# Attention stage of a two-layer local-attention kernel: VectorE instructions issued without a wait for their own completion

## The reference

```python
def _layer(x, wqkv, qs, ksc, wo, lg, lb, w1, b1, w2, b2):
    h = shift_token(x)
    q, k, v = jnp.split(h @ wqkv, 3, axis=-1)      # to 8 heads of 64
    q = l2norm(q) * qs; k = l2norm(k) * ksc
    q, k = rotary_xpos(q, k)
    o = local_attention(q, k, v)                   # softmax(q k^T + mask) v
    x = x + o @ wo
    h = layernorm(shift_token(x)) @ w1 + b1
    a, g = jnp.split(h, 2, axis=-1)
    return x + (a * gelu(g)) @ w2 + b2
```

## Time and profile before

| | us |
|---|---|
| median of three runs | 2925.17 |
| lowest, highest | 2924.01, 2929.32 |
| the profiled execution, its own time | 2930.93 |
| its span on the slowest core (core 4) | 2929.4 |
| spans of the eight cores | 2912.0 to 2929.4 |
| TensorE busy | 2051.2 (70%) |
| VectorE busy | 1078.7 (37%) |
| ScalarE busy | 590.3 (20%) |

### The profile page before, as it was taken

The page is one execution under the profiler, slowest core; times in us unless marked ns, Lnnn a source line. Parts: engine busy times, 40 slices in busy tenths (PEclk is TensorE's granted clock), DMA queues, the critical chain, the costliest instruction groups (busy, mean ns, idle before and its releaser), DMA issues.

```text
span 2929.4 us, 27366 instructions; the slowest of 8 cores (2912.0 to 2929.4 us)
## 1 busy us (share of the span) xinstructions
PE 2051.2 (70%) x9366; PEld 931.7 (32%) x9488; DVE 1078.7 (37%) x1849; ACT 590.3 (20%) x1016; POOL 35.5 (1%) x50
## 2 busy tenths in 40 slices
PE   1167576799775674999225777758997767659993
PEld 1122232344322341444112233323442333314442
DVE  5705445311135446111373344453111444462113
ACT  1132331210022322110012233302100323311100
POOL 0000000000010000000000000000000000000000
PEclk9986556799885556999557855568998755579996
DMA  4239930121259800222332300001213200002223
GB/s 94 72 46 101 111 46 29 36 80 55 46 67 111 96 11 26 72 65 72 115 108 37 43 1 1 1 29 51 75 58 41 36 1 1 1 29 72 63 73 109
DMA packets 123852, 159.70 MB, mean 55 GB/s; under 512 B 48211, under 2 KB 90708, under 8 KB 122500
## 3 DMA queue, kind: packets, MB, share of 16 engines
q0 software_dynamic: 30624, 52.42, 15.4%
q1 hardware_dynamic: 93092, 105.53, 12.6%
HBM read 201.95 MB, written 44.03 MB: 84 GB/s over the span
## 4 chain that ended last, share of the span: by engine, by line
PE 60%; DVE 20%; ACT 6%; issue 5%; DMA 5%; SPq 3%; DVEq 1%; ACTq 0%
PE psA L1627 11%; PE psA L1185 8%; DVE UN L337 8%; PE psA L1610 5%; PE psA L1606 5%; PE psB L1610 5%; PE psB L1606 5%; DVE Bb L337 4%; DVE attnT L337 4%; PE psB L963 4%; PE psA L874 4%; PE psB L1224 3%; DMA out<-UN 2%; PE psA L1337 2%; PE psB L874 2%
## 5 line engine op out<-in xcount | busy, mean ns | idle before, releaser
L337 ACT ACT_TABLE_LOAD x67 | 86.0, 1283 | 1170.3 <-PE psA L1185 369.1
L1610 PE MATMUL psB<-stg,WS 128*128 128x512 bf16 x704 | 277.0, 393 | 24.6 <-ACT stg L337 23.2
L1606 PE MATMUL psB<-stg,WS 128*128 128x512 bf16 x672 | 263.7, 392 | 28.8 <-ACT stg L337 28.8
L1610 PE MATMUL psA<-stg,WS 128*128 128x512 bf16 (+1 forms) x704 | 268.9, 382 | 1.3
L1606 PE MATMUL psA<-stg,WS 128*128 128x512 bf16 (+1 forms) x680 | 260.5, 383 | 0.0
L1627 PE MATMUL psA<-Bb,WS 128*128 128x512 bf16 x1000 | 229.9, 386 | 14.0 <-DVE UN L337 12.9
L1185 PE MATMUL psA<-Bb 64*128 64x128 bf16 (+3 forms) x432 | 179.3, 415 | 34.5 <-ACT probs L337 29.7
L337 ACT ACTIVATE probs<-psA 128x640 bf16<-128x640 f32 (+5 forms) x264 | 171.4, 649 | 94.6 <-PE psA L1185 69.1
L1224 PE MATMUL psB<-attnT,Bb 128*64 128x128 bf16 x960 | 79.1, 311 | 145.5 <-DVE attnT L337 145.5
L337 DVE TENSOR_TENSOR UN<-UN 128x1024 bf16<-128x1024 bf16 (+1 forms) x48 | 41.7, 870 | 323.5 <-ACT UN L337 284.9
L874 PE MATMUL psA<-stg,WS 128*128 128x512 bf16 x502 | 133.8, 426 | 31.7 <-DMA WS<-wqkv 22.7
(11 more groups left out here) (118 smaller groups left out, 2435.6 us busy)
## 6 DMA issues: line engine op xcount, KB each, us to landing
WS<-wpre SPq DMA_DIRECT2D x184, 256.0 KB, 2.8
wpre<-w1p POOLq DMA_DIRECT2D x8, 2730.0 KB, 71.0
WS<-wpre SPq DMA_DIRECT2D x96, 224.0 KB
UN<-x SPq DMA_DIRECT2D x32, 512.0 KB, 4.5
WS<-wqkv POOLq DMA_DIRECT2D x24, 512.0 KB, 5.8
wpre<-w2p POOLq DMA_DIRECT2D x4, 2730.0 KB, 145.1
out<-UN SPq DMA_DIRECT2D x16, 512.0 KB, 5.2
Bb<-c_tabhi SPq DMA_DIRECT2D x8, 512.0 KB
```

Source lines behind the costliest of these rows:

```text
L337: ins = f(*a, **kw)
L1606: t.matmul(rA[0:ln, tc * 512:(tc + 1) * 512], wu[:, kt * ln:(kt + 1) * ln], B.stg[kt][:, tc * 512:(tc + 1) * 512], start=(kt == 0), stop=( ...
L1610: ins = t.matmul(rG[0:ln, tc * 512:(tc + 1) * 512], wu[:, 1024 + kt * ln:1024 + (kt + 1) * ln], B.stg[kt][:, tc * 512:(tc + 1) * 512], sta ...
```

## The change

In `phase_attn` four kinds of VectorE instruction are issued through `B.Vn` in place of `B.V`: the norm of the even head of each pair, both od casts of the pairs 0 to 2, the copy into `attnT[0]` of every pair, and od1 of the last pair. Unchanged on `B.V` are the reciprocals, the norms of the odd heads, the copies into `attnT[1]` and od2 of the last pair. No instruction with data is added, removed or moved, and no wait for another engine is touched.

```diff
                     for hh in (2 * pj, 2 * pj + 1):
-                        ev = B.ev(B.sV, v.tensor_scalar_mul(
+                        vv = B.Vn if hh % 2 == 0 else B.V
+                        ev = B.ev(B.sV, vv.tensor_scalar_mul(
                             B.probs[:, hh * 640:hh * 640 + w],
                             B.probs[:, hh * 640:hh * 640 + w],
                             B.rcp[:, hh:hh + 1]))
...
                     if pj >= 1:
                         B.w(v, "vector", av_pred[pj - 1])
-                        v.tensor_copy(
+                        B.Vn.tensor_copy(
                             B.odm(pj - 1)[0:64, qc * 128:(qc + 1) * 128],
                             B.psB[0:64, 1024:1152])
-                        ev = B.ev(B.sV, v.tensor_copy(
+                        ev = B.ev(B.sV, B.Vn.tensor_copy(
                             B.odm(pj - 1)[64:128, qc * 128:(qc + 1) * 128],
                             B.psB[64:128, 1536:1664]))
...
-                    ev = B.ev(B.sV, v.tensor_copy(
+                    ev = B.ev(B.sV, B.Vn.tensor_copy(
                         B.attnT[0][:, 0:w],
                         B.psB[:, 0:w // 2].bitcast(BF16)))
...
                 B.w(v, "vector", av_pred[3])
-                v.tensor_copy(B.odm(3)[0:64, qc * 128:(qc + 1) * 128],
-                              B.psB[0:64, 1024:1152])
+                B.Vn.tensor_copy(B.odm(3)[0:64, qc * 128:(qc + 1) * 128],
+                                 B.psB[0:64, 1024:1152])
```

## The result

The change makes the kernel faster: 2880.5 us median of ten runs against 2925.9 for the kernel before on the same chips, ratio 0.9841 with a 95% interval of 0.9831 to 0.9852, so 43 to 49 us less. Executions in which the cores of one die show a lower clock take some per cent longer and are left out of all ratios and intervals. The forecast was 2874 with a range of 2864 to 2896. On another chip the same kernel gave 0.982 (0.980 to 0.984).

A forecast was written before the change was run, and what follows sets the result against it. In attention, VectorE's string of two od casts and two attnT copies sets each round, TensorE's transposes close behind. Terms 34.3 + 15.5 + 1.0 + 0.4 = 51 us, giving a median of 2874, range 2864 to 2896.

The forecast's parts named there:

- Price of a wait: VectorE instructions directly behind each other: removing the wait between them saves a 0.105 gap plus 0.083 overlap, 0.19 us.
- The wait for TensorE is passed early: Before attnT copies, VectorE's queue passes the satisfied TensorE wait while the previous instruction runs: 0.25 us, at worst 0.08.
- The od casts 0.30 apart: od1 to od2, on different partitions, start 0.30 us apart (0.39 before): no gap and no overlap.
- TensorE limits the wide rounds: Five key blocks: transposes hold attnT[0] till 0.77 and attnT[1] till 1.29 us after AV's end; round 0.33 shorter.
- the sign that the prediction gave: In the timeline after the change, attnT[0] would be shown as released by TensorE (L1199), and attnT[1] too.
- Narrow blocks: Eight blocks of fewer key blocks, where transposes are not the limit: 0.50 us a round, 15.5 us in all.
- The sum, 51 us: Whole kernel: 34.3 wide blocks, 15.5 narrow blocks, 1.0 norms of the narrowest blocks, 0.4 last od2 before output projection.
- the terms: Saving in one block of five key blocks: 0.44 us at its head plus three rounds of 0.33.
- The late wait: Rival, chance 0.22: TensorE's wait before attnT is looked at only after completion; 33 us, 2892, or 2895 without norm overlap.
- no gain: Rival, chance 0.05: what the removed VectorE waits cost must be paid in any case; price 0, time 2925.
- The clock in attention: Rival, chance 0.04: TensorE's clock rises above 0.50 in attention; 2775, or 2800 to 2860 in some phases only.
- Instructions in flight together: Rival, chance 0.03: overlapping instructions stretch each other, attnT copies 0.49 to 0.69 us; at 0.25 more, 2937.

The follow-up runs named there:

- the norms alone: Kernel before, with only the norms of the even heads issued without their own wait; time ratio to before 0.9971 (0.9943 to 1.000) in the second run.
- attnT[0] alone: Kernel before, with only the copy into attnT[0] issued without its own wait; time ratio to before 0.989 (0.987 to 0.991).
- the kernels with all norms: Whole change plus odd-head norms without their own wait: ratio to before 0.981; with the od casts of all four pairs in swapped order too: 2868.0 us, 0.9785.
- the change once more: The whole change, unaltered, run again on this chip against the kernel before: ratio 0.982, median core's span 2920.4 to 2868.5 us.
- the parts alone: Kernel before with only one kind freed of its own wait: even norms (ratio 0.9971), attnT[0] copies (0.989) or od casts (0.993).

## Why the prediction held, and where its sizes were off

- **Price of a wait, 0.19 directly behind each other.** Right: the norms went from 0.88 to 0.68 for a pair, and the norms alone gave the 7 us forecast.
- **The wait for TensorE is passed early, 0.25.** Right: copies at the head of a block from 1.15 to 0.89, 34.8 us for attnT[0] alone.
- **The od casts 0.30 apart.** Measured 0.31, and 0.33 from od2 to attnT[0]. The prediction gave the Trainium skill's rule on held instructions ("VectorE: DVE Perf Modes", section "Two Vector instructions with no wait between them") for neighbours only. The section says more: an input from PSUM is compared with the last instruction that read PSUM, however far back. That is what the kernels with all norms showed (0.04 behind where the last such instruction was od2, 0.08 of overlap where it started at partition 0). The same page's section "The DRAIN you can't avoid", which measured eight copies as equally long with and without semaphores between them, does not fit here: 480 waits less, 53.9 us less.
- **TensorE limits the wide rounds, 0.33 gained.** Right, 0.34: attnT[1] began 1.29 after the end of AV (1759.67 - 1758.38), as worked out. attnT[0] began at 0.75, where the prediction had 0.77 by its transposes. Its row names no releaser, against the sign that the prediction gave, because od2 ends at the same moment; but it stays there with the casts swapped and with the casts on ScalarE (0.76), so it is the transposes. That both limits meet so closely is chance.
- **Narrow blocks, 0.50 a round.** Measured 0.49 for one key block in the rows shown (2.05 to 1.56), and 0.48 in the median for each of the four widths.
- **The sum, 51 us.** The phases lost 53.9. A wide block's period went from 24.13 to 22.65 us, 1.48, where the terms said 1.43: 24 x 0.05 = 1.2 of the difference of 3; the rest was not traced.
- **From the phases to the time.** Here the size was off the other way: 46 us by the ratio of the first runs, 53 by that of the change once more (0.982), against 51. The spans outside the phases scatter by core and execution by more than this difference, and the profiles show no stage that got longer. Whether a few us are given back in some executions stays open.
- **The rivals.** The late wait and no gain are out by the parts alone. (The late wait was worked out to 2892 to 2895, not quite the 2896 that closes the range.) The clock in attention stayed at 0.50; the means over the whole span were 0.753 to 0.756 before and 0.757 to 0.758 after, which fits a shorter stretch at 0.50. Instructions in flight together did not stretch: attnT copies of five blocks have a mean of 490 ns, before 492.

## What to carry to other kernels

Where two neighbouring VectorE instructions have no data in common, a wait for one's own completion between them costs the gap and, where both start at the same partition, the overlap, here 0.19 to 0.25 us. It counts only where VectorE's string is what another engine waits for. Before adding up such gains, work out when the other engine's own work would release each step: the three parts here were worth 63.9 us alone and 53.9 together. And once waits are gone, look at the order of instructions on different partitions: swapping two casts gave 2.5 us here, and 5.8 with all norms, at no cost.

## What the runs showed of the hardware that was not expected

- A cast on partitions 64 to 127 costs the overlap of the next PSUM read from partition 0, even when a run of scores and several SBUF instructions lie between: 0.12 us a block in 28 of 32 blocks of the kernel with all norms, absent in the four without such a cast in front, and gone with the swap.
- A second wait in front of a matmul group, on another engine's semaphore, came with 0.11 us more from VectorE's end to the matmul (0.25 against 0.14), more than moving two casts to an idle ScalarE gave: the phases grew by 7.3 us. The wait was satisfied by then and stood second in TensorE's queue.
- A row can hide its releaser: 0.04 us of idle time and no name, and yet eight transposes in place of ten let attnT[1] start 0.13 earlier.
